# A graph transformer block: a new hand-written order of all engines, and the first group turned on the matrix engine

## The reference

```python
def _ln(x, g, b):
    mu = jnp.mean(x, axis=-1, keepdims=True)
    var = jnp.mean((x - mu) ** 2, axis=-1, keepdims=True)
    return (x - mu) * jax.lax.rsqrt(var + EPS) * g + b
b, s, d = x.shape                      # 128, 128, 256; H = 8 heads of HD = 32
nx = _ln(x, ln1_g, ln1_b)
q, k, v = nx @ wq + bq, nx @ wk + bk, nx @ wv + bv      # each split into 8 heads
bias = jnp.where(adj > 0, 0.1 * adj * adjf, -jnp.inf)[:, None]
scores = jnp.einsum('bhqd,bhkd->bhqk', q, k) / np.sqrt(HD) + bias
attn = jax.nn.softmax(scores, axis=-1)
out = jnp.einsum('bhqk,bhkd->bhqd', attn, v)
x1 = x + (out @ wo + bo)
n2 = _ln(x1, ln2_g, ln2_b)
return x1 + gelu(n2 @ w1 + b1) @ w2 + b2                # w1 256x1024, w2 1024x256
```

## Time and profile before

| | |
|---|---|
| median of three runs | 1379.5 us |
| the profiled execution | 1382.0 us, of which the span is 1380.2 us |
| TensorE busy | 1329.0 us (96% of the span), 11356 matmuls |
| VectorE, ScalarE, GpSimd busy | 1138.2 us (82%), 1150.8 us (83%), 643.5 us (47%) |
| chain that ended last | TensorE 92% |
| granted clock over 40 slices | 0.6, 0.8, 0.6 and then 0.9 or more |

### The profile page before, as it was taken

One profiled execution on the slowest core, in us unless ns is written; L12 is line 12 of the kernel. 1 busy time (PEld: TensorE's weight loads), 2 busy tenths in 40 slices (PEclk: granted clock), 3 DMA queues, 4 the chain that ended last, 5 costly groups with the idle time before them and its releaser, 6 DMA issues.

```text
span 1380.2 us, 33642 instructions
## 1 busy us (share of the span) xinstructions
PE 1329.0 (96%) x11356; PEld 1144.2 (83%) x11356; DVE 1138.2 (82%) x1970; ACT 1150.8 (83%) x3336; POOL 643.5 (47%) x617
## 2 busy tenths in 40 slices
PE   3868999999999999999999999999999999999999
PEld 3647888888888888888888888888888888888878
DVE  2689888898888888888888888888888888888762
ACT  2659888898889889888889888888988888898764
POOL 5445455444555544545554454554445555444110
PEclk6869999999999999999999999999999999999999
DMA  5345554555555465565446556545555554554330
GB/s 175 131 130 176 169 166 147 171 164 159 171 167 155 147 181 153 150 187 166 142 152 182 149 159 186 158 143 164 169 150 171 173 154 148 176 160 132 126 111 32
DMA packets 170307, 213.85 MB, mean 155 GB/s; under 512 B 16144, under 2 KB 149520, under 8 KB 170256
## 3 DMA queue, kind: packets, MB, share of 16 engines
q1 hardware_dynamic: 170256, 213.20, 50.9%
HBM read 112.47 MB, written 100.66 MB: 154 GB/s over the span
## 4 chain that ended last, share of the span: by engine, by line
PE 92%; ACT 2%; DVE 2%; DMA 2%; POOL 1%; issue 1%; SPq 0%; DVEq 0%; ACTq 0%
PE work L403 29%; PE work L404 25%; PE work L405 25%; PE area L461 6%; PE work L482 5%; PE work L507 2%; DMA moved_flat<-flat 1%; ACT xhat L698 1%; DMA probt<-moved_blocks 1%; ACT soft L635 0%; POOL xt_lo L1074 0%; PE work L410 0%; DVE flat L956 0%; DMA wa_raw<-in_L_gnn_wq 0%; ACT qk_all L685 0%
## 5 line engine op out<-in xcount | busy, mean ns | idle before, releaser
L635 ACT ACTIVATE soft<-soft,nmax 128x128 f32<-128x128 f32 x1024 | 396.6, 393 | 51.2 <-DVE nmax L855 50.8
L403 PE MATMUL work<-w_hi,hid_parts 128*128 128x256 f32 x1024 | 288.7, 282 | 0.0
L404 PE MATMUL work<-w_lo,hid_parts 128*128 128x256 f32 x1024 | 285.3, 279 | 0.0
L405 PE MATMUL work<-w_hi,hid_parts 128*128 128x256 f32 x1024 | 285.2, 279 | 0.0
L1074 POOL TENSOR_TENSOR xt_lo<-xraw,xt_hi 128x512 fp32r<-128x512 f32 x64 | 82.5, 1291 | 295.2 <-ACT xt_hi L665 295.2
L403 PE MATMUL work<-nt_hi,w_hi 128*128 128x512 f32 x512 | 207.4, 405 | 0.5 <-DVE nt_lo L947 0.5
L964 DVE TENSOR_TENSOR hid_parts<-late_memory,hid_parts 128x512 fp32r<-128x512 f32 x256 | 193.0, 763 | 14.0 <-ACT hid_parts L730 12.4
L720 ACT ACTIVATE late_memory<-work,b_col 128x512 f32<-128x512 f32 x256 | 174.2, 680 | 35.5 <-PE work L405 35.0
L404 PE MATMUL work<-nt_lo,w_hi 128*128 128x512 f32 x512 | 200.5, 392 | 0.0
L405 PE MATMUL work<-nt_hi,w_lo 128*128 128x512 f32 x512 | 200.0, 391 | 0.0
L403 PEld LDWEIGHTS work<-w_hi,hid_parts 128*128 128x128 f32 x1024 | 192.1, 188 | 4.8
(11 more groups left out here) (94 smaller groups left out, 3094.2 us busy)
## 6 DMA issues: line engine op xcount, KB each, us to landing
moved_blocks<-wa_raw SPq DMA_DIRECT2D x128, 512.0 KB, 3.0
probt<-moved_blocks SPq DMA_DIRECT2D x512, 128.0 KB, 3.1
xin<-in_x SPq DMA_DIRECT2D x32, 512.0 KB, 6.1
moved_flat<-flat SPq DMA_DIRECT2D x32, 512.0 KB, 3.0
xraw<-moved_flat SPq DMA_DIRECT2D x128, 128.0 KB, 3.5
out<-res SPq DMA_DIRECT2D x128, 128.0 KB, 4.1
adj_in<-in_adj SPq DMA_DIRECT2D x32, 256.0 KB, 3.1
res<-in_L_gnn_w SPq DMA_DIRECT2D x1, 1024.0 KB, 9.8
```

What stands on the lines that cost most here:

```text
L403: pe.matmul(o, lhs_hi, rhs_hi, start=first, stop=False)
L404: pe.matmul(o, lhs_hi, rhs_lo, start=False, stop=False)
L405: return pe.matmul(o, lhs_lo, rhs_hi, start=False, stop=last)
L635: a = act.activation(soft[:, b % 2, h, :], soft[:, b % 2, h, :], ACT.Exp, bias=nmax[:, b % 2, h:h + 1], accum_out=rsum[:, b % 2, h:h + 1])
```

## The change

The bodies of SyncE, TensorE, ScalarE and VectorE get a new order; GpSimd's stays. The order of TensorE puts `score` and `mix` side by side in four places, where before there were six places with one of them and one with both. `values(.., 0)` and `score(.., 0)` of a group move to the end of the step before. `UNITS` follows, with other banks. For the first group alone the trip through DRAM is left out: TensorE transposes it (`first_turn`), ScalarE takes the hi part from PSUM and VectorE the lo part (`first_lo`), in place of `flat_blocks`, `send_flat`, `fetch_flat`, `rows_lo`. Parts of the diff that repeat the pattern are cut.

```diff
 LAND = RPB * 16
 
 
-UNITS = [("v", 0, 0, 0), ("nt", 0, -2, 1), ("nt", 1, -2, 2), ("down", 2, -3, 0), ("down", 3, -3, 1),
-         ("mix", 1, -1, 3), ("up", 0, -2, 2), ("up", 1, -2, 0), ("up", 2, -2, 1), ("proj", 1, -1, 3),
-         ("up", 3, -2, 2), ("up", 4, -2, 0), ("mix", 2, -1, 3), ("v", 1, 0, 1), ("up", 5, -2, 2),
-         ("up", 6, -2, 0), ("proj", 2, -1, 3), ("up", 7, -2, 1), ("mix", 3, -1, 3), ("qk", 0, 1, 2),
-         ("proj", 3, -1, 3), ("down", 0, -2, 0), ("qk", 1, 1, 1), ("down", 1, -2, 2), ("mix", 0, 0, 3),
-         ("qk", 2, 1, 0), ("qk", 3, 1, 1), ("proj", 0, 0, 3)]
+UNITS = [("nt", 0, -2, 1), ("nt", 1, -2, 2), ("proj", 0, -1, 3), ("down", 3, -3, 0), ("mix", 1, -1, 3),
+         ("up", 0, -2, 2), ("up", 1, -2, 1), ("up", 2, -2, 0), ("proj", 1, -1, 3), ("up", 3, -2, 2),
+         ("up", 4, -2, 1), ("mix", 2, -1, 3), ("up", 5, -2, 2), ("up", 6, -2, 0), ("up", 7, -2, 2),
+         ("v", 1, 0, 1), ("proj", 2, -1, 3), ("down", 0, -2, 0), ("mix", 3, -1, 3), ("qk", 0, 1, 2),
+         ("qk", 1, 1, 1), ("proj", 3, -1, 3), ("qk", 2, 1, 2), ("qk", 3, 1, 0), ("v", 0, 1, 1),
+         ("down", 1, -2, 2), ("mix", 0, 0, 3), ("down", 2, -2, 0)]
 PLACE = {(kind, i): at for at, (kind, i, _, _) in enumerate(UNITS)}
 PER_GROUP = {"down": GB, "v": 2, "qk": 4, "up": FC, "nt": DC, "mix": GB, "proj": GB}
...
             def send_flat(step, off):
-                if not step.has(off):
-                    return
-
-                sp.wait_ge(flat_ready, step.through(off, 1, 0))
+                if not step.has(off) or step.at_first(off):
+                    return
+
+                sp.wait_ge(flat_ready, step.through(off - 1, 1, 0))
                 sp.dma_start(moved_flat.rearrange("i k j n -> (i k) (j n)"),
                              flat[:, :, :, :].rearrange("p j m t -> p (j m t)")).then_inc(flat_sent, 16)
 
...
             sp.dma_start(w2_raw, w2.rearrange(chunked, p=P)).then_inc(w2_loaded, 16)
 
             def body(step):
-                send_blocks(step, -1, 2)
                 send_flat(step, 1)
                 fetch_blocks(step, -1, 2)
                 send_blocks(step, -1, 3)
                 fetch_flat(step, 1)
                 load_x(step, 2)
+                store(step, -3, 0)
                 fetch_blocks(step, -1, 3)
-                store(step, -3, 0)
+                send_blocks(step, 0, 0)
                 store(step, -3, 1)
-                store(step, -3, 2)
-                send_blocks(step, 0, 0)
                 fetch_blocks(step, 0, 0)
                 load_adj(step, 2)
+                store(step, -3, 2)
                 send_blocks(step, 0, 1)
+                fetch_blocks(step, 0, 1)
+                send_blocks(step, 0, 2)
                 store(step, -3, 3)
-                fetch_blocks(step, 0, 1)
 
             steps(sp, groups, body)
...
+            def first_turn():
+
+                for c in range(DC):
+                    for b in range(GB):
+                        if c == 0:
+                            pe.wait_ge(xhat_ready, b + 1)
+                        mm = pe.transpose(work[:, c, b * P:(b + 1) * P], xhat[:, b, c * P:(c + 1) * P], ident[:, :])
+                    mm.then_inc(first_turned, 1)
+
+            early_columns()
+            first_turn()
 
             def flip(step, off, c):
                 if not step.has(off):
...
@@ -569,11 +581,9 @@
                 mm.then_inc(full["down"], 1)
 
             def body(step):
-                values(step, 0, 0)
                 flip(step, -2, 0)
                 flip(step, -2, 1)
-                score(step, 0, 0)
-                down(step, -3, 2)
+                project_out(step, -1, 0)
                 down(step, -3, 3)
                 score(step, 0, 1)
                 mix(step, -1, 1)
@@ -584,23 +594,25 @@
                 up(step, -2, 3)
                 up(step, -2, 4)
                 mix(step, -1, 2)
-                values(step, 0, 1)
+                score(step, 0, 2)
                 up(step, -2, 5)
                 up(step, -2, 6)
+                up(step, -2, 7)
+                values(step, 0, 1)
                 project_out(step, -1, 2)
-                score(step, 0, 2)
-                up(step, -2, 7)
+                down(step, -2, 0)
                 mix(step, -1, 3)
+                score(step, 0, 3)
                 query_key(step, 1, 0)
-                score(step, 0, 3)
+                query_key(step, 1, 1)
                 project_out(step, -1, 3)
-                down(step, -2, 0)
-                query_key(step, 1, 1)
+                query_key(step, 1, 2)
+                query_key(step, 1, 3)
+                values(step, 1, 0)
                 down(step, -2, 1)
                 mix(step, 0, 0)
-                query_key(step, 1, 2)
-                query_key(step, 1, 3)
-                project_out(step, 0, 0)
+                score(step, 1, 0)
+                down(step, -2, 2)
 
             steps(pe, groups, body)
...
+                if step.at_first(off):
+                    act.wait_ge(first_turned, c + 1)
+                    act.activation(xt_hi[:, c, :], work[:, c, :], ACT.Copy).then_inc(hi_taken["xt"], 1)
+                    return
+                act.wait_ge(flat_landed, step.through(off - 1, 1, 0, LAND))
                 act.activation(xt_hi[:, c, :].rearrange("p (b i t) -> p b i t", b=GB, i=RPB),
...
                 gelu(step, -2, 1)
@@ -750,32 +764,36 @@
                 hidden_hi(step, -2, 3)
                 attn_hi(step, -1, 2)
                 gelu(step, -2, 4)
-                rows_hi(step, 1, 0)
                 hidden_hi(step, -2, 4)
                 gelu(step, -2, 5)
                 hidden_hi(step, -2, 5)
-                values_copy(step, 0, 1)
-                rows_hi(step, 1, 1)
                 gelu(step, -2, 6)
                 hidden_hi(step, -2, 6)
                 gelu(step, -2, 7)
+                hidden_hi(step, -2, 7)
+                rows_hi(step, 1, 0)
+                values_copy(step, 0, 1)
+                rows_hi(step, 1, 1)
+                exponential(step, 0, 1, 1)
                 attn_hi(step, -1, 3)
-                hidden_hi(step, -2, 7)
-                exponential(step, 0, 1, 1)
...
+                    dve.tensor_tensor(xt_lo[:, c, :], work[:, c, :], xt_hi[:, c, :].bitcast(F32),
+                                      ALU.subtract).then_inc(taken["xt"], 1)
+
             def flat_blocks(step, off):
-                if not step.has(off):
-                    return
-                need(dve, flat_sent, step.through(off - 1, 1, 0, 16))
+                if not step.has(off) or step.at_first(off):
+                    return
+                need(dve, flat_sent, step.through(off - 2, 1, 0, 16))
                 need(dve, taken["xt"], step.through(off - 1, DC, DC - 1))
...
                                   res[:, par, b, :], ALU.add).then_inc(taken["down"], 1)
 
             def body(step):
-                maximum(step, -1, 3)
-                flat_blocks(step, 1)
+                result(step, -3, 2)
                 flip_lo(step, -2, 0)
-                add_edges(step, 0, 0)
                 residual(step, -1, 0)
-                result(step, -3, 2)
                 maximum(step, 0, 0)
                 flip_lo(step, -2, 1)
+                invert(step, -1, 3)
                 result(step, -3, 3)
-                invert(step, -1, 3)
+                flat_blocks(step, 1)
                 normalise(step, -1, 3)
+                attn_lo(step, -1, 1)
                 turn_blocks(step, -1, 3)
-                attn_lo(step, -1, 1)
+                invert(step, 0, 0)
+                stats2_of(step, -1, 0)
                 add_edges(step, 0, 1)
+                residual(step, -1, 1)
+                hidden_lo(step, -2, 0)
+                hidden_lo(step, -2, 1)
+                hidden_lo(step, -2, 2)
                 maximum(step, 0, 1)
-                invert(step, 0, 0)
-                hidden_lo(step, -2, 0)
-                residual(step, -1, 1)
-                hidden_lo(step, -2, 1)
-                stats2_of(step, -1, 0)
                 normalise(step, 0, 0)
-                attn_lo(step, -1, 2)
-                hidden_lo(step, -2, 2)
-                turn_blocks(step, 0, 0)
-                stats2_of(step, -1, 1)
                 hidden_lo(step, -2, 3)
                 hidden_lo(step, -2, 4)
+                attn_lo(step, -1, 2)
+                turn_blocks(step, 0, 0)
+                hidden_lo(step, -2, 5)
+                hidden_lo(step, -2, 6)
+                add_edges(step, 0, 2)
                 residual(step, -1, 2)
-                add_edges(step, 0, 2)
-                hidden_lo(step, -2, 5)
+                maximum(step, 0, 2)
+                stats1(step, 2)
+                hidden_lo(step, -2, 7)
+                attn_lo(step, -1, 3)
+                stats2_of(step, -1, 1)
                 stats2_of(step, -1, 2)
-                hidden_lo(step, -2, 6)
-                attn_lo(step, -1, 3)
-                stats1(step, 2)
```

(62 more changed lines are left out.)

1 line of the change is left out of this document (removed).

## The result

The changed kernel takes 1423.2 us, the median of runs from 1422.05 to 1424.23, beside 1380.2 us for the kernel before in the same runs. The ratio is 1.0318, with a 95% interval from 1.0298 to 1.0338. It is 43 us slower; the forecast was 1408.5, 28 us slower, with a range up to 1438. The profiled execution took 1424.2 us, of which the span is 1422.4. The file is 26 lines longer, so numbers of lines shift: the `hidden_lo` of L964 is now L990, the `residual` of L904 is L922, `flip` of L507 is L519.

A forecast was written before the change was run, and what follows sets the result against it. TensorE, without idle time in its 40.55 us steps, was taken as the bound. Changes -18, start -12, wait +49 and clock +10 gave +29 on the profiled 1382.0: 1411.0, or 1408.5 us against the median, range 1388 to 1438.

The forecast's parts named there:

- Changes between tile and full products: TensorE's order: four stretches of tile products per step instead of seven, 0.20 us each, 18 us gained.
- The wait: TensorE's first down piece waits for hidden_lo(-2, 7), queued behind residual, maximum and statistics: 1.75 us in 28 steps, +49 us.
- the two extras: Behind the wait: 0.06 us until TensorE starts and 0.10 for the first product's delay; without them 1.55 us, 43 us.
- The clock: Behind the new wait the clock falls one time in five: 6 x 1.7 = 10 us, ends 0 and 48.
- three products away from a mix and score pair lies between the two kinds: The new 1.75 us wait placed between waits with half clock behind them and one without; hence one fall in five.
- The start: First group turned on TensorE: first product 14.9 us sooner, of which 12 us gained, ends 5 and 16.
- `flat_blocks(1)` would come late: VectorE reaches the second group's flat_blocks only behind maximum(0, 0) and late_rows; that group is turned only 5.8 us sooner.
- the old start has waits of its own which the new list doesn't have: Reason given for taking 12 us gained at the start although the second group is only 5.8 us sooner.
- The rival without the wait: Rival one: no wait at chunk 7 of the first down piece, gains of changes and start stay: 1349.5 us; chance 0.11.
- The rival with a fall at every wait: Rival two: the clock falls at every new wait, 48 us in place of 10: 1446.5 us; chance 0.10.
- The rival of a change inside the pair: Rival three: tile pairs of two kinds cost a change inside, 1417.5 us, or 1426.5 with a whole change; chance 0.12.
- waits elsewhere: Rival four: VectorE or a fetch is late elsewhere too; with another 1 us per step 1437 us; chance 0.09.

The follow-up runs named there:

- the split pair: The first experiment's kernel with score(0, 2) taken out of its pair with mix and put between two up pieces; 1357.4 us.
- the first experiment: The changed kernel with hidden_lo(-2, 7) moved ahead of residual(-1, 2) on VectorE; 1349.1 us, ratio 0.9772 to the kernel before.
- the turned order: The first experiment's kernel with late_hi and late_lo moved into step 1, plus score ahead of mix in all four pairs; 1338.9 us, ratio 0.9708.
- the last experiment: The first experiment's kernel with late_hi and late_lo moved into step 1, plus GpSimd's residual_start cut to 8 of 256 columns from the third group; 1338.7 us.

## Why the prediction was right, and where its sizes were off

Against the medians, 1380.2 to 1423.2, three of the four terms now have measured sizes, and the fourth is what they leave. The main term was right in its mechanism. The errors of the terms are -4, +4, +10 and +4 us; the first two cancel, and the rest makes the 14.7 by which the time lies above the forecast.

- *Changes between tile and full products*: forecast -18, measured -22 (0.73 us in 30 steps). The rows around one lone score gave 0.20 for a stretch; the split pair gave 0.26. The term was undersized because the rows of one place were taken for all seven. Going in from transposes, for one, costs more: from the first of eight transposes to the score behind them it was 0.97 us (592.47 to 593.44 in the trace of the kernel before), to a projection it is 0.79 (577.21 to 578.00 in that of the first experiment).
- *The wait*: forecast +49, measured 41.70 - 39.82 = 1.88 us in 28 steps, +53. The mechanism, the place and the three durations were right to 0.05 us each. The rest is that the residual starts 0.20 to 0.30 behind the projection's end by turns, because VectorE comes there with no time to spare, where the forecast gave it 0.2 us. And full products of 256 columns here came 0.113 us apart, so that chunk 7 was due sooner. Two small slips of the working change nothing: without the two extras the wait is 4.06 - 2.47 = 1.59 and not 1.55, and VectorE's idle time is 5.3 us per step by the earlier trace rows, above the "4 to 5".
- *The clock*: forecast +10, with 6 falls; measured about 12 x 1.6 = 20. The price of a fall was right (1.7 against 1.6), their number was not. This is the largest error of a term. The step that failed is "three products away from a mix and score pair lies between the two kinds": I took the distance of three products for some protection, and they gave little: with them the clock fell in 12 of 27 steps, with a piece of 1.4 us added to them in 1 of 27.
- *The start*: forecast -12, not measured by itself. What the other terms leave is 43 + 22 - 53 - 20 = -8, and this remainder also holds the ends and the fall of the clock in step 2, about +2; so start and ends bring some 10, near the 9 of the first experiment. The profiles split it: at the transposes of step 2 the changed kernel is 10.4 us ahead (97.68 against 108.09). In the first experiment, where it is 9.5, step 2 then takes 2.4 longer than before and what lies behind the last full step 5.2 less, as it fits the `down` piece that moved. That `flat_blocks(1)` would come late was right. Missing was `late_lo`: it ran in 7.7 us in place of 5.1, beside GpSimd's addition of the residual (59.91 to 63.23), and the projection's bank waited for the residual behind it. My 12 rested on "the old start has waits of its own which the new list doesn't have"; the new list had a longer one.

By construction the four add up to +43. The rival without the wait was wrong as a forecast for this kernel, but its time, 1349.5, is that of the first experiment to half a microsecond; that closeness is luck, as the larger gain of the changes and the smaller one of the start cancel. The rival with a fall at every wait was half true. The rival of a change inside the pair is refuted by the split pair and the turned order. Of waits elsewhere there were none of weight in the steady part: of its 44.8 us without TensorE, 44.0 are for `hid_parts`. The rule of the Trainium skill, TensorEngine Tiling (Array Packing), Key Properties, is that a change of mode drains the engine. It agrees with what going in and out costs (0.26 us), and not with what was seen for row tiles next to column tiles: mix takes 0.57 us to score and score 0.65 to a full product, and neither splitting nor reordering shows a cost inside the pair.

What stays open: where the border lies between a wait that lowers the clock and one that doesn't, and why it falls in some steps and not in others with the same wait. It isn't the small differences of the wait: in the changed kernel waits of 1.57 and 1.66 us alternate from 296 us on, and the clock falls behind both, four times and six times, every second or third step. That `late_lo` was slowed by GpSimd's addition is read from the rows and from what the last experiment showed for `normalise`; it was not tested by itself.

## What to carry to other kernels

When the order of a full engine is rearranged, walk each wait of the new list from its last common cause, here the projection's end, on both engines, and add up what stands in the queue of the other engine before the awaited piece: 4.1 us against 2.5 was to be read from the old trace and cost more than all gains. Put an operation that someone waits for ahead of those nobody waits for. Keep waits away from tile products: the same 1.6 us cost another 1.6 in 12 of 27 steps where such products stood close behind it, and almost nothing more with a piece of full products between.

## What was not expected of the hardware

- A wait of 1.6 us, 0.55 us ahead of 1.2 us of tile products, lowered the clock in 12 of 27 steps; the same wait with 1.4 us of full products between in 1 of 27; a wait of 0.9 us never; 2.25 us in 20 of 27.
- VectorE's operation with two SBUF inputs stood still for the rest of a GpSimd addition that had begun before it: 2.96 us in place of 1.21.
- The distance of full products of 256 columns isn't one number: 0.113 us in the `down` piece above (587.30 to 589.56 are 20 distances), 0.12 in `values` and 0.118 in most of the kernel before.
